# Decoder block on one core: earlier loads of head-group stacks in the cross-attention units

## The reference, cut to what matters

```python
x = x + _L0_attn_ref(...)    # A0: causal attention with rope, 16 heads of 8
x = x + _L0_xattn_ref(...)   # X0: cross attention to a context of 77 tokens, 16 heads of 8
x = x + _L0_ffn_ref(...)     # M0: 8 experts, two chosen for each token
x = x + _L1_attn_ref(...)    # A1: attention without a mask, 16 heads of 8
x = x + _L1_xattn_ref(...)   # X1: cross attention with one head of 128
x = x + _L1_ffn_ref(...)     # F1: linear layer, convolution over three tokens, silu, linear layer

# inside _L0_xattn_ref
q = _split_heads(Q @ Wq + bq); k = _split_heads(K @ Wk + bk); v = _split_heads(V @ Wv + bv)
attn = jax.nn.softmax(jnp.einsum('bhqd,bhkd->bhqk', q, k) * scale, axis=-1)
out = jnp.einsum('bhqk,bhkd->bhqd', attn, v)
return out.transpose(0, 2, 1, 3).reshape(Q.shape[0], -1, D) @ Wo + bo
```

## Time and profile before

| what | value |
|---|---|
| median of three runs | 866.35 us (865.83 to 869.03) |
| the profiled execution, its own time | 866.97 us |
| its span | 864.8 us |
| mean granted TensorE clock | 0.859 of full speed |
| PE busy | 703.1 us, 81% |
| DVE busy | 591.5 us, 68% |
| ACT busy | 415.3 us, 48% |
| POOL busy | 284.2 us, 33% |

### The profile page before, as it was taken

The page is one execution under the profiler, slowest core; times in us unless marked ns, Lnnn a source line. Parts: engine busy times, 40 slices in busy tenths (PEclk is TensorE's granted clock), DMA queues, the critical chain, the costliest instruction groups (busy, mean ns, idle before and its releaser), DMA issues.

```text
span 864.8 us, 14952 instructions
## 1 busy us (share of the span) xinstructions
PE 703.1 (81%) x4698; PEld 338.7 (39%) x4698; DVE 591.5 (68%) x1606; ACT 415.3 (48%) x708; POOL 284.2 (33%) x504
## 2 busy tenths in 40 slices
PE   2489999989899889308999992459799998999787
PEld 1245454444344344205666661213233232324443
DVE  3757678676646564636787872588889898962664
ACT  1314565555754444002333330308688877886454
POOL 4624444544522123741332331121423034230220
PEclk9767999999975666758999996658999999999898
DMA  7533664382222212411111113520222211000000
GB/s 214 192 125 112 193 183 132 122 270 76 68 81 58 81 47 76 125 55 29 41 41 44 42 35 106 170 74 25 67 82 86 86 43 34 26 2 1 0 25 25
DMA packets 74780, 71.27 MB, mean 82 GB/s; under 512 B 14560, under 2 KB 67168, under 8 KB 74704
## 3 DMA queue, kind: packets, MB, share of 16 engines
q1 hardware_dynamic: 72000, 64.84, 24.5%
q0 software_dynamic: 2272, 4.69, 1.7%
q10 hardware_dynamic: 432, 0.79, 0.2%
HBM read 41.90 MB, written 28.00 MB: 81 GB/s over the span
## 4 chain that ended last, share of the span: by engine, by line
PE 61%; DVE 20%; issue 7%; ACT 4%; DMA 4%; POOL 2%; DVEq 1%; SPq 1%; another core or an unknown queue 1%; POOLq 0%; ACTq 0%
PE bank_pv L732 11%; DVE mx L590 9%; PE bank_turn L574 7%; PE bank_scores L2018 5%; PE bank_scores L684 4%; PE bank_scores L1768 4%; PE bank_turn L1753 4%; PE bank_scores L1753 4%; PE bank_turn L751 3%; PE bank_scores L1761 2%; PE bank_turn L793 2%; PE bank_turn L528 2%; DVE xn L471 1%; DMA stk<-stack_A 1%; PE bank_turn L578 1%
## 5 line engine op out<-in xcount | busy, mean ns | idle before, releaser
L590 DVE TENSOR_REDUCE mx<-bank_turn 128x1 f32<-128x512 f32 (+3 forms) x452 | 260.6, 616 | 73.5 <-PE bank_turn L579 35.6
L574 PE MATMUL bank_turn<-stk 64*128 64x77 bf16 (+4 forms) x708 | 165.0, 316 | 31.4 <-DVE mx L590 20.2
L684 PE MATMUL bank_scores<-stk 64*128 64x512 bf16 (+4 forms) x576 | 179.1, 378 | 4.8 <-ACT probs L705 3.6
L709 ACT ACTIVATE probs<-bank_scores 128x1024 f32<-128x1024 f32 (+4 forms) x160 | 117.5, 768 | 108.0 <-PE bank_scores L684 106.1
L705 ACT ACTIVATE probs<-bank_scores 128x512 f32<-128x512 f32 x256 | 138.6, 605 | 35.5 <-PE bank_scores L684 34.5
L732 PE MATMUL bank_pv<-probs,vsl 128*32 128x512 f32 (+4 forms) x1152 | 148.7, 591 | 2.8 <-POOL probs L717 1.9
L574 PEld LDWEIGHTS bank_turn<-stk 64*128 64x128 bf16 x708 | 55.2, 103 | 137.4 <-DVE mx L590 65.7
L717 POOL TENSOR_SCALAR_AFFINE_SELECT probs<-probs 128x256 f32<-128x256 f32 x128 | 52.1, 410 | 80.5 <-ACT probs L709 79.1
L1736 POOL DMA_INDIRECT expert_outputs<-probs,y_at x39 | 37.4, 960 | 108.8 <-DVE probs L1655 105.9
L528 PE MATMUL bank_turn<-ident,xn 128*128 128x128 f32 x60 | 14.4, 384 | 63.0 <-DVE xn L471 63.0
L477 POOL TENSOR_TENSOR rstd<-var,mhalf 128x4 f32<-128x4 f32 x24 | 25.4, 1058 | 119.2 <-DVE var L456 118.9
(11 more groups left out here) (299 smaller groups left out, 1191.3 us busy)
## 6 DMA issues: line engine op xcount, KB each, us to landing
stk<-stack_A SPq DMA_DIRECT2D x64, 256.0 KB, 3.3
w<-in_M_w SPq DMA_DIRECT2D x12, 512.0 KB, 4.5
stack_A<-parts SPq DMA_DIRECT2D x15, 384.0 KB, 3.0
stack_A<-fill SPq DMA_DIRECT2D x8, 512.0 KB, 5.6
stk<-stack_X SPq DMA_DIRECT2D x16, 256.0 KB, 2.7
stack_A<-parts SPq DMA_DIRECT2D x15, 256.0 KB, 3.2
probs<-routed_tokens SPq DMA_DIRECT2D x39, 65.0 KB, 1.8
b_gated<-in_M_b SPq DMA_DIRECT2D x1, 2048.0 KB, 11.4
```

The source lines that it names most:

```text
L574: mm = e.matmul(o, stk[r, slot, 0, pp, qt * P:(qt + 1) * P], stk[r, slot, 1, pp, 0:keys], start=True, stop=not a.causal)
L590: e.tensor_reduce(o.rearrange("p h q -> p q h"), bank_of((g, m))[:, 0:k * keys].rearrange("p (q h k) -> p q h k", q=len(tiles), h=len(hs)) ...
L684: mm = e.matmul(score_bank(g, kt, i)[0:a.kp, 0:S - q0], stk[r, slot, 1, pp, kt * P:kt * P + a.kp], stk[r, slot, 0, pp, q0:S], start=True, ...
L709: e.activation(probs[0:a.kp, probs_of(g, kt), j:HG:2, 0:n], bank_scores[0:a.kp, 2 * j:2 * j + 2, 0:n], ACT.Exp, scale=1 / math.sqrt(HD)).t ...
```

## The change

SP's order in the cross units is altered in two ways; no other engine's instructions change.

Part one: in a cross unit g SP issues the load of unit g+4 in place of that of unit g+3, still at the head of the unit and so ahead of the shift of unit g+2. The load of unit 19, which no cross unit would then issue, is put at the end of unit 15, behind the shifts of units 16 and 17. As unit 16 used to begin with that load, its place in SP's order is the same as before.

Part two: the stack DMAs of cross queries whose split is done in a cross unit (16 and 22) are issued in that unit, behind its shift, and no longer in the next unit. Splits done in units of A0 keep their place.

```diff
         def unit_sp(e, g):
-            if UNITS <= g % (2 * UN) + 3 and g + 3 <= last_of_stream(g):
-                load_sp(e, g + 3)
+            ahead = UNITS if layer(g) is X0 else UNITS - 1
+            if UNITS <= g % (2 * UN) + 3 and g + ahead <= last_of_stream(g):
+                load_sp(e, g + ahead)
             if layer(g) is not X0:
                 for t in turned_in(g):
                     shift_sp(e, t)
             if X0.first - 1 <= g <= last_of_stream(X0.first) - 2:
                 shift_sp(e, g + 2)
-            if g - 1 in SPLIT_IN:
+            if g == X0.first - 1:
+                load_sp(e, X0.first + UNITS - 1)
+            if g - 1 in SPLIT_IN and layer(g - 1) is not X0:
                 stack_dma(e, *SPLIT_IN[g - 1])
+            if g in SPLIT_IN and layer(g) is X0:
+                stack_dma(e, *SPLIT_IN[g])
```

## The result

The changed kernel takes 860.79 us (median of 12 runs, 853.32 to 868.09) against 865.89 us for the kernel before (12 runs, 857.27 to 869.70). The ratio is 0.9938 with a 95% interval of 0.9912 to 0.9965: 5.1 us faster by the medians. Measured twice more, the same kernel gave 0.9944 and 0.9964; the mean of the three is 0.9949, or 4.4 us. Both kernels scatter by 12 to 15 us from run to run, far more than the three first runs of before (865.83 to 869.03) let one expect. The ratios leave out single runs that lay far above the others: 868.09 us here, 869.89 and 869.15 us of the changed kernel later, 876.75 us of the kernel before, and 947.85 and 1541.92 us in two of the experiments; the medians keep them.

A forecast was written before the change was run, and what follows sets the result against it. The prediction took PE, at 1.2 GHz in much of the cross units, as the bound, with load waits at units 17 and 25. It summed -2.08 + 0 + 0 + 0.5 = -1.6 us to 864.8 us, range 861.0 to 868.5 us.

The forecast's parts named there:

- The load of unit 27: Start of unit 25: issued a unit earlier, the load lands before PE wants it; all of PE's 2.08 us wait goes.
- Unit 19's load: Start of unit 17: the load stays behind the same two shifts, so PE's 0.90 us wait stays.
- contention: Around unit 16: the load of unit 20 shares DMA engines with that of unit 19; taken as 0, at most 0.9 us.
- the shifts: Cross units: shifts behind the moved loads are issued at most 0.1 us later; cost nothing, tightest cover 1.7 us at unit 25.
- Part two: Units 16 and 22: earlier stacks cost nothing; alone they leave some 0.3 of 2.08 us, with the loads moved add nothing.
- The rest of the cross units isn't held by loads: Cross units outside the starts of units 17 and 25: PE at 1.2 GHz bounds, busy 37.10 of 37.10 us from 249.2 us.
- The term for the clock: Behind the removed gap: work moved earlier may run at half clock, costing 0 to 1.04 us; taken as +0.5 us.
- the clock better by a unit: Rival: the missing idle time or new alignment keeps one more unit at 2.4 GHz, 3.9 us, giving 860.9 us; chance 0.17.
- The clock worse by a unit: Rival: the rise at 313.6 or 340.9 us is missed, +3.9 us, 868.7 us, chance 0.12; two missed, 872.6 us, chance 0.05.

The follow-up runs named there:

- stacks alone: Kernel before with only the stack DMAs of units 16 and 22 issued in their own unit, loads in their old places: 866.65 us, ratio 1.0006.
- before again: The kernel before measured again with no edit: 868.93 us, ratio 1.0008.
- load 27 alone: Kernel before with only the load of unit 27 moved, from the head of unit 24 to the head of unit 23: 866.04 us, ratio 1.0000.
- load 23 put back: Changed kernel with only the load of unit 23 returned to the head of unit 20, behind the shift of unit 21: 864.03 us, ratio 0.9993.
- after again and third: The changed kernel measured a second and a third time with no edit: 863.19 and 861.60 us, ratios 0.9944 and 0.9964.
- loads 23, 27 and 31 alone: Kernel before with only the loads of units 23, 27 and 31 moved a unit ahead: 862.38 us, ratio 0.9962.
- loads alone: Changed kernel with the stack DMAs back in their old places, measured twice (the second called again): 864.00 and 860.44 us, ratios 0.9979 and 0.9945.
- load 19 alone: Kernel before with only the load of unit 19 moved ahead of the shift of unit 17 in unit 15: 863.82 us, ratio 0.9993.
- the version without any wait for a load: Changed kernel with the load of unit 19 also ahead of the shift of unit 17, measured twice: 856.06 and 855.91 us, ratios 0.9892 and 0.9908.

## Why the prediction was right, and where it failed

**The load of unit 27: right.** Its wait of 2.08 us went as a whole. Alone it is worth 2.5 us of the stretch in one profile each, though the measured ratio of 1.0000 (0.9974 to 1.0026) doesn't show it.

**Unit 19's load, contention, the shifts: right.** The wait before unit 17 is 0.98 to 1.01 us after and 0.90 to 1.02 us before, so the load of unit 20 on its heels costs nothing measurable. L684 waited for no shift in the cross units. One count was wrong without weight in the sum: the change issues earlier only the 12 loads of units 20 to 31, not all 16.

**Part two: right with part one, wrong alone.** With part one it adds nothing that these runs can tell. For the stacks alone I had said that some 0.3 us of the wait would be left. In fact the order of SP only changed the load that suffers, and waits of 2.64 and 1.92 us took the place of the one of 2.08 us.

**The step that failed: "The rest of the cross units isn't held by loads".** It was read from one execution, in which the clock stood at half level from 249.2 to 286.3 us. With units 19 and 20 at that level PE is slow enough to hide this late load, by less than 1 us. The sentence was true of that execution and not of the kernel: in the second profile of the same kernel the clock rose at 265.3 us, and PE waited 1.99 us for the load of unit 23. That load stands behind the late shift of a unit with moments in DVE just as the load of unit 27 does. I had found the pattern at unit 25 and hadn't asked where else it recurs, every fourth unit. The profile I had could have warned me. With this load late and that of unit 27 early the ratios were 1.0000 and 0.9993, with both early 0.9955 in the mean of six. So, as far as these runs tell, the surplus comes from this wait, which the forecast put at nothing: 1.08 to 2.32 us itself where it shows, and the clock behind it.

**The term for the clock: wrong sign.** I had +0.5 us, the middle between levels that stay where they are while work moves and levels that move with it. The stretch went from 112.3 us (mean of two profiles) to 105.6 us (mean of 107.06, 105.40 and 104.37), 6.7 us. PE's busy time in it, for the same matmuls, went from a mean of 94.8 us (96.56, 93.00) to 90.3 us (92.55, 88.85, 89.35). So by these five profiles 4.5 us of the 6.7 are clock and 2.2 are idle time. They show the place. Where the wait before unit 21 fell into a full-level stretch, in three kernels (before again, load 27 alone, load 23 put back), that stretch ended after 10.2 us. Where the level rose at a like place and there was no such wait (after again and third, loads 23, 27 and 31 alone, and the loads alone), it held for 23.9 us. The wait isn't the only thing that ends it: in the first profile after, with the stacks alone and with load 19 alone the level rose at 261 to 264 us and fell after 6.8 us with no wait for a load inside, and with the loads alone, again, it stayed at half to 280 us. The Trainium skill, "TensorE: Matmul & The Clock Gate", section "HAM oscillation — how this bites in real kernels", describes a kernel in which TensorE waits some 3 to 5 us for a DMA between two groups of matmuls, and the next group starts with the clock throttled. These traces agree in kind, and the fall comes behind shorter waits, of 1.08 to 2.32 us.

**The rival that came nearest** was the clock better by a unit, 860.9 us at a chance of 0.17. Its time is that of the first measurement, which is partly luck: the mean of three is 4.4 us below before and not the 5.5 us that it stands for. Its cause was wrong in place: with the gap before unit 25 gone alone, the level behind it fell and rose about as before (0.50 from 292 to 313 us), while the kernels with the load of unit 23 early and those with it late differ in the level around unit 21.

**The clock worse by a unit.** The rise at 313.6 us was indeed missed in all three profiles of the changed kernel, with the clock at half for 47.6 to 47.8 us from 285 to 289 us on, and the kernel was faster all the same. It was missed in the second profile of the kernel before too, so the change can't be named as the cause.

**What stays open.** The level in one execution can't be forecast: the first profile after had no wait before unit 21 and yet a full stretch of only 6.8 us. The profiles of the stretch give 6.7 us where the three ratios give 4.4 us; with two and three profiles of kernels that scatter by 15 us, that difference isn't settled. The part of the span behind the stretch, which holds the same instructions, took 508.0 and 507.8 us before and 503.6, 510.7 and 505.2 us after. And whether part two is worth anything up to 0.3% wasn't told apart.

## What to carry to other kernels

A view of waits is the view of one alignment of the clock. When a wait is found behind some order of a queue, look for every other place with the same order, and ask of each how much cover it has, and whether a faster engine would uncover it; profile the unchanged kernel two or three times before pricing an edit.

A stall of 1 to 2 us in front of TensorE can cost more than itself when the clock falls behind it, and taking the last one away can be worth more than the first: the version without any wait for a load is 8.0 to 9.4 us faster than before, for waits of 3.0 and 4.6 us in the two profiles of before. Its stretch is 10.1 us shorter than before's, and what lies behind the stretch is as long (507.0 and 508.9 us).

In SP's written order, moving an item can hand its delay to the neighbour: the stacks alone did so to the loads of units 20 and 26, the load of unit 19 alone to that of unit 20. It needn't: the loads of units 27, 23 and 31 moved without it. Look at who stands behind the moved item; moving the whole row by one step was safe here.

## What the runs showed that I hadn't expected

- The kernel before, unchanged, gave 857 to 873 us over these runs, with the mean granted clock of an execution between 0.85 and 0.88. The three runs within 865.83 to 869.03 us had suggested 0.4%.
- PE was busy for 37.10 of 37.10 us at 1.2 GHz without the level rising, and the level rose in other executions in the same units at 261 to 265 us. What decides it these runs don't show.
- The mean granted clock doesn't tell the time by itself. The load of unit 19 alone had 0.868 over its 12 runs, the changed kernel 0.867 to 0.868 in its three measurements, and yet load 19 alone showed no gain; its profile has waits of 5.3 us in the cross units, those of the changed kernel 1.0 us.
